# A two-stage attention and expert kernel: new order of loads and first chain, and batches with a Newton reciprocal and ScalarE's work in another order

## Chip, cores and metric

One Trainium2 chip, one of its cores. The metric is the device time of one execution in microseconds (us), the median of several runs. The engines are TensorE (PE), VectorE (DVE), ScalarE (ACT), GpSimd (POOL) and SyncE (SP), which only starts transfers here.

## The reference

Sixteen sequences of 512 tokens, 128 channels, all fp32. The first half is linear attention with random features, the second a feed-forward layer that sends each token to one of eight experts. Both are gated by rows made from a 16 x 128 condition.

```python
mod = silu(c) @ wmod                       # 6 rows per sequence: sa, ca, ga, sb, cb, gb
h = layernorm(x) * (1 + ca) + sa
q, k = feature(h @ Wq.T + bq), feature(h @ Wk.T + bk)   # exp(proj - norm) + 1e-6, 32 per head, 16 heads
kv, ksum = k.T @ v, sum(k)                 # per head
x = x + ga * ((q @ kv) / (q @ ksum) @ Wo.T + bo)
h = layernorm(x) * (1 + cb) + sb
e = argmax(h @ gate_W + gate_b)            # one expert of 8 per token
x = x + gb * (gelu(h @ W1[e] + b1[e]) @ W2[e] + b2[e])
```

The division by `q @ ksum` is the part of the arithmetic that the change writes in another way.

## The kernel before

Each engine has its own instruction list, written out by hand in program order, and waits on semaphores. There is no scheduler: an engine does its list in order, and whatever stands behind a waiting instruction waits too.

**Head.** SP starts the first loads (L324 to L332). ACT and DVE make silu of the condition (L494, L669 to L673), PE multiplies it with `wmod` (L973 to L976), DVE turns the products into columns `sa`, `ca1` (L685, L686) and rows `modrow` (L687 to L704), which go through DRAM and come back copied to all partitions as `modb` (L340, L335).

**Sixteen batches**, one for each sequence (`over_batches`, L89). In batch b:

- ACT (L546 to L572): four exponentials of the k features (`kf`, L531), with the copy of h2 of batch b-2 (`h2T`, L540), the copy of v (L527) and the copy of the gate logits (`lgT`, L544) among them; four exponentials of the q features (`qf`, L536), with the modulated input `hT` of batch b+1 (L509) after the second; k and its squares for batch b+1 (L516, L517), the copy `kvm` (L565), q and its squares (L522, L523), the denominator `den` (L570), and last the normalised input `xn1` of batch b+2 (four instructions, L503). In the profile `kvals`, `ksqs`, `hT`, v and `xn1` are all parts of one tile, `shared`.
- PE (L1125 to L1152): k features (L1016, L1019), transposes of h2 (L1084), v (L1000), gate (L1091), output projection of batch b-1 (L1076), q features (L1028, L1031), transposes of `xn1` of batch b+1 (L987), the key-value product (L1042, L1046), the k projection of b+1 (L995), ranks of b-2 (L1106 to L1109), two transposes (L1053), the q projection of b+1 (L995), and `attend` (L1060 denominator, L1064 numerator).
- DVE (L867 to L904): residual and statistics, expert choice and slots of b-2, scaling of h2 of b-1, and last `attention` (L718): a RECIPROCAL of `den` (L720), then `oT` = numerator times reciprocal (L723).
- POOL (L444 to L456): for even b the first layer norm's scale and shift of the pair b+2, b+3 (`rstd1_of`, L411 and L413), the second layer norm's scale of b-1 (`rstd2_of`, L419, which also waits for the gate rows of batch b-2), `gated` (L421: `wo`, `bog`, and the bias added to x, L427 to L434), which waits for `den` of batch b, and four indirect DMAs that scatter the rows of b-2 to lists of their experts in DRAM (L440).
- SP: gate rows of each batch copied into the payload tiles `pay` (`gate_rows`, L362, L366). They stand behind all loads of x, the late `modb` rows, `firsts`, `w2` and the padding (L343 to L352).

**Last batch.** PE first counts the tokens of the experts (`count`, L1117) and transposes a table of blocks (L1122) ahead of the q features; DVE makes that table (L868 to L872).

**Experts.** 71 blocks of 128 tokens: load, transpose (L1168), first product (L1175), gelu (L594), second product (L1188), bias, gate and residual on DVE (L921 to L926), and an indirect DMA out (L473). The last two batches' choice of experts runs among the first 32 blocks.

## Time and profile before

| what | value |
|---|---|
| median of 3 runs | 429.49 us (427.32 to 431.19) |
| the profiled execution's own time | 431.88 us |
| its span on the core | 430.0 us |
| busy share PE / DVE / ACT / POOL | 87% / 70% / 63% / 47% |
| granted clock of TensorE, mean | 0.97 |

The span is what the trace shows, from the first instruction to the last; 1.9 us of the execution's own time lie around it. The batches take roughly the stretch from 17 to 258 us, the experts the rest. Times in the views are microseconds from the start of the span unless marked ns. A busy PE is not PE at its peak, since matmuls are pipelined.

### The profile page before, as it was taken

Reading aid. Unit: us, or ns where it says so; the run is one execution under the profiler, and the core shown is the slowest. Engines: PE = TensorE matmul, PEld = TensorE weight load, DVE = VectorE, ACT = ScalarE, POOL = GpSimd, SP = SyncE. Lnnn points to the kernel's source line nnn. Section 1 sums busy time; section 2 is a strip of 40 time slices with the busy share of each in tenths; the row PEclk is TensorE's granted clock in tenths of the full one; section 3 lists DMA queues with packets and bytes.
Section 4 is the critical chain, followed back from the end, with each engine's and each line's share of the span. In section 5 each row is a group of like instructions: output and inputs, shape, how many; then the busy total and the mean of one; then the engine's idle time right before and its main releaser. Section 6 shows DMA issues by size and latency. Waiting matters only on the chain.

```text
span 430.0 us, 12990 instructions
## 1 busy us (share of the span) xinstructions
PE 373.3 (87%) x4487; PEld 284.5 (66%) x4487; DVE 300.8 (70%) x1106; ACT 272.9 (63%) x710; POOL 201.6 (47%) x226
## 2 busy tenths in 40 slices
PE   3598959999999999999999977998787899999990
PEld 1354636565655565565556537987787799999990
DVE  3536858987988898879867878777365566665651
ACT  2676754787687669667776726654554376657660
POOL 1210334553843664565546425455546354554452
PEclk9999998999999999999999989999898899999996
DMA  6458962112211221221122147344434455554410
GB/s 199 158 188 320 374 187 101 58 45 101 79 63 64 96 81 40 88 99 57 49 101 76 57 134 224 96 108 141 149 113 146 140 187 182 147 147 121 123 32 2
DMA packets 30782, 52.38 MB, mean 122 GB/s; under 512 B 4194, under 2 KB 22758, under 8 KB 30336
## 3 DMA queue, kind: packets, MB, share of 16 engines
q1 hardware_dynamic: 24352, 34.50, 26.5%
q0 software_dynamic: 6368, 17.05, 10.9%
q8 instruction: 38, 0.62, 0.6%
q14 instruction: 24, 0.20, 0.1%
HBM read 28.46 MB, written 19.34 MB: 111 GB/s over the span
## 4 chain that ended last, share of the span: by engine, by line
PE 55%; ACT 17%; DVE 13%; issue 7%; another core or an unknown queue 3%; DVEq 2%; DMA 1%; POOL 1%; POOLq 0%; SPq 0%; ACTq 0%
PE ps_proj L1188 10%; PE ps_feat L1175 6%; PE ps_proj L1028 4%; PE ps_proj L995 4%; DVE rden L720 4%; PE ps_out L1076 3%; PE ps_den L1060 3%; PE ps_proj L1031 3%; ACT kf L531 3%; PE ps_kv L1175 3%; PE ps_feat L1016 3%; PE ps_den L1175 3%; ACT qf L536 3%; ACT shared L516 2%
## 5 line engine op out<-in xcount | busy, mean ns | idle before, releaser
L473 POOL DMA_INDIRECT out<-kf,modb x71 | 70.6, 995 | 75.2 <-DVE kf L926 67.3
L1188 PE MATMUL ps_proj<-w2sb,qf 128*128 x568 | 77.1, 281 | 0.0
L440 POOL DMA_INDIRECT experts_lists<-pay,slot x64 | 63.5, 992 | 17.6 <-issue 17.6
L1188 PEld LDWEIGHTS ps_proj<-w2sb,qf 128*128 128x128 f32 x568 | 71.3, 197 | 0.0
L586 ACT ACTIVATE xT<-ps_out 128x128 f32<-128x128 f32 x71 | 19.7, 278 | 62.5 <-PE ps_out L1168 45.0
L720 DVE RECIPROCAL rden<-den 128x512 f32<-128x512 f32 x16 | 53.6, 3351 | 5.6 <-ACT den L570 5.3
L921 DVE TENSOR_TENSOR kf<-ps_proj,firsts_sb 128x128 f32<-128x128 f32 x71 | 20.7, 291 | 51.0 <-PE ps_proj L1188 22.9
L536 ACT ACTIVATE qf<-ps_proj 128x512 f32<-128x512 f32 x32 | 17.4, 595 | 45.8 <-PE ps_feat L1031 45.8
L427 POOL TENSOR_TENSOR wo<-wsb,modb 128x128 f32<-128x128 f32 x16 | 7.5, 469 | 82.3 <-ACT den L570 82.3
L1175 PE MATMUL ps_feat<-xT,shared 128*128 128x128 f32 x288 | 39.6, 281 | 5.4 <-ACT xT L586 3.6
L594 ACT ACTIVATE qf<-ps_feat,shared 128x128 f32<-128x128 f32 x144 | 41.0, 376 | 0.0
L1175 PEld LDWEIGHTS ps_feat<-xT,shared 128*128 128x128 f32 x288 | 35.9, 196 | 6.8 <-issue 6.2
L995 PE MATMUL ps_proj<-shared,wsb 128*128 128x512 f32 x64 | 34.2, 619 | 2.2 <-ACT shared L509 1.4
L861 DVE COPY shared<-firsts_sb 128x516 f32 x71 | 31.8, 448 | 2.5 <-issue 2.3
L1016 PEld LDWEIGHTS ps_feat<-feat_w,shared 32*128 32x128 f32 x256 | 19.7, 186 | 14.3 <-issue 14.2
L503 ACT ACTIVATE shared<-xall,shift,rstd 128x128 f32<-128x128 f32 x64 | 26.2, 481 | 4.0 <-POOL shift L413 4.0
L419 POOL TENSOR_TENSOR rstd<-ve,mhalf 128x4 f32<-128x4 f32 x16 | 16.6, 1036 | 25.1 <-DVE ve L621 11.9
L1016 PE MATMUL ps_feat<-feat_w,shared 32*128 32x128 f32 x256 | 26.7, 283 | 1.7 <-ACT qsqs L523 1.7
L1016 PE MATMUL ps_proj<-feat_w,shared 32*128 32x128 f32 x256 | 26.5, 283 | 0.0
L1175 PE MATMUL ps_den<-xT,shared 128*128 128x128 f32 x144 | 19.8, 282 | 6.4 <-ACT xT L586 3.5
L1019 PE MATMUL ps_feat<-csb,shared 32*128 32x128 f32 x256 | 25.1, 270 | 0.0
L1019 PE MATMUL ps_proj<-csb,shared 32*128 32x128 f32 x256 | 24.9, 270 | 0.0
(177 smaller groups left out, 965.1 us busy)
## 6 DMA issues: line engine op xcount, KB each, us to landing
modb<-experts_lists SPq DMA_DIRECT2D x71, 196.0 KB
xall<-in_x SPq DMA_DIRECT2D x16, 256.0 KB, 2.9
pay<-modb SPq DMA_DIRECT2D x16, 256.0 KB, 2.6
modb<-modulation_rows SPq DMA_DIRECT2D x1, 3072.0 KB, 11.0
firsts_sb<-in_firsts SPq DMA_DIRECT2D x1, 2576.0 KB, 16.9
experts_lists<-padding SPq DMA_DIRECT2D x9, 196.0 KB
out<-kf,modb POOLq DMA_INDIRECT x71
modb<-modulation_rows SPq DMA_DIRECT2D x1, 1024.0 KB, 5.1
```

The lines of the kernel that those rows point to most:

```text
L440: g_.indirect_dma_start(out=lists, in_=pay[b.home][:, t, :], in_offset=None, out_offset=bass.IndirectOffsetOnAxis(ap=slot[b.home][:, t:t + ...
L473: g_.indirect_dma_start(out=rows_out, in_=yb[u], in_offset=None, out_offset=bass.IndirectOffsetOnAxis(ap=token, axis=0), bounds_check=last ...
L503: ins = a.activation(xn1[:, t, :], xall[:, b.v * LT + t, :], ACT.Identity, bias=shift1[:, at:at + 1], scale=rstd1[:, at:at + 1])
L536: a.activation(qf[:, Q_ORDER[n], :], QB[Q_ORDER[n]][:, :], ACT.Exp).then_inc(s_exp, 1)
L594: ins = a.activation(g[k % R4][:, c * P:(c + 1) * P], HID[k % R4][:, c * P:(c + 1) * P], ACT.Gelu, bias=firsts_c[k % R4][:, WB1 + c:WB1 + ...
L720: v.reciprocal(rden[:], den[:]).then_inc(s_rden, 1)
L861: v.tensor_copy(firsts_c[k % R4], firsts_sb[:, bass.ds(expert[k] * WB, WB2)]).then_inc(s_fc, 1)
L995: mm(PJ[i][:, :], wsb[:, i * P:(i + 1) * P], hT[:], start=True, stop=True).then_inc(s_proj, 1)
L1016: mm(QB[c][:, tokens], kvals[at, tokens], feat_w[at, :], start=True, stop=False)
L1019: ins = mm(QB[c][:, tokens], ksqs[at, tokens], norm_w[at, :], start=False, stop=True)
L1175: ins = mm(HID[u % R4][:, c * P:(c + 1) * P], firsts_c[u % R4][:, c * P:(c + 1) * P], xT[u % 2][:], start=True, stop=True)
L1188: ins = mm(Y[u % 2][:, 0:D], g[u % R4][:, c * P:(c + 1) * P], w2sb[:, bass.ds(e * DFF + c * D, D)], start=(c == 0), stop=(c == FC - 1))
```

## The change

It has two halves. In the head: x of the first batch is loaded before the weights; PE runs 48 idle matmuls ahead of the condition's products and 12 more before the first projection; the column products come first and have a semaphore of their own; the first `xn1` is made half by ACT and half by DVE, the second by DVE alone; the first q projection goes into another bank, so that the first k features need no q; gate rows of batches 0 to 2 are copied before most loads of x, and `w2` is loaded last, behind the gate rows of batch 3.

In the batches: `den` becomes a logarithm, an exponential of its negative gives a first value of the reciprocal, and DVE makes one Newton step of it in two instructions (with the sign turned, so the residual subtracts). ACT makes `xn1` of batch b+1 after the four k exponentials of batch b, no longer that of b+2 at the end; `h2T` is copied one exponential earlier, `kvm` ahead of the squares of k. POOL's `rstd1_of` goes from the front of an even batch to its end. In the last batch count and table transpose go later on PE.

```diff
@@ sync @@
+            load_x(0, 0)
             sp.dma_start(wsb[:], weights).then_inc(s_w, 16)
-            load_x(0, 0)
...
-            with sp.Fori(EARLY_ROWS // 2, B // 2) as i:
-                for parity in range(2):
-                    sp.wait_ge(s_x[parity], 16 * i)
-                    load_x(2 * i + parity, parity)
+            load_x_behind(EARLY_ROWS)
+            load_x_behind(EARLY_ROWS + 1)
+            sp.wait_ge(s_mb, 16)
+            sp.wait_ge(s_pset, 2 + HOMES)
+            for v in range(HOMES):
+                gate_rows(v)
+            load_x_behind(EARLY_ROWS + 2)
+            load_x_behind(EARLY_ROWS + 3)
             load_rows(EARLY_ROWS, B, s_mbl)
+            for b in range(EARLY_ROWS + 4, B):
+                load_x_behind(b)
             sp.dma_start(firsts_sb[:], firsts).then_inc(s_w1, 16)
+            sp.wait_ge(s_pset, 3 + HOMES)
+            sp.dma_start(lists[PADROW:PADROW + P, :], padding[:]).then_inc(s_pad, 16)
+            sp.wait_ge(s_mbl, 16)
+            gate_rows(HOMES)
             sp.dma_start(w2sb[:, :].rearrange("p (e c d) -> p e c d", e=E, c=FC),
                          w2.rearrange("e (c p) d -> p e c d", p=P)).then_inc(s_w2, 16)
@@ gpsimd @@
-                if ahead and b.par == 0:
-                    rstd1_of(b.half + 3, b=b + 2)
                 if not first:
                     rstd2_of(b + -1, rows_of=None if second else b + -2)
                 gated(b, first)
                 if not first and not second:
                     scatter(b + -2)
+                if ahead and b.par == 0:
+                    rstd1_of(b.half + 3, b=b + 2)
@@ scalar @@
+            a.preload_act_table_set("natural_log_exp_and_others")
...
                 k_feature(b, 0)
-                k_feature(b, 1)
                 if not first and not second:
                     h2T_copy(b + -2)
+                k_feature(b, 1)
...
                 k_feature(b, 3)
+                if not first and not last:
+                    normalise1(b + 1)
                 q_feature(b, 0)
...
                 if not last:
-                    k_parts(b + 1)
-                act.wait_ge(s_kvt, b.v + 1)
-                a.activation(kvm[:], G[:, 0:2 * P], ACT.Copy).then_inc(s_kvm, 1)
+                    k_values(b + 1)
+                kvm_copy(b)
                 if not last:
+                    k_squares(b + 1)
                     q_parts(b + 1)
                 act.wait_ge(s_den, b.v + 1)
                 act.wait_ge(s_eps, b.v + 1)
-                a.activation(den[:], G[:], ACT.Identity, bias=kveps[:, 1:2]).then_inc(s_denp, 1)
-                if b.v + 2 < B:
-                    normalise1(b + 2)
+                a.activation(den[:], G[:], ACT.Ln, bias=kveps[:, 1:2]).then_inc(s_denp, 1)
+                act.wait_ge(s_denp, b.v + 1)
+                a.activation(rden[:], den[:], ACT.Exp, scale=-1.0).then_inc(s_rden, 1)
@@ vector @@
-                dve.wait_ge(s_denp, b.v + 1)
-                v.reciprocal(rden[:], den[:]).then_inc(s_rden, 1)
                 dve.wait_ge(s_rden, b.v + 1)
+                v.scalar_tensor_tensor(out=G[:], in0=G[:], scalar=kveps[:, 1:2], in1=rden[:],
+                                       op0=ALU.add, op1=ALU.mult).then_inc(s_rdst, 1)
+                dve.wait_ge(s_rdst, 2 * b.v + 1)
+                v.scalar_tensor_tensor(out=rden[:], in0=G[:], scalar=2.0, in1=rden[:],
+                                       op0=ALU.subtract, op1=ALU.mult).then_inc(s_rdst, 1)
@@ tensor @@
+            pe.wait_ge(s_set, 3)
+            keep_busy(48)
             pe.wait_ge(s_silu, 1)
...
-                if last:
-                    count(0)
                 k_features(b, first)
...
                 v_project(b)
+                if last:
+                    count(0)
...
-                if last:
-                    table_transpose(0)
...
                 if not last:
                     transpose_xn(b + 1, first)
+                else:
+                    table_transpose(0)
```

`load_x_behind(b)` waits until x of batch b-2 has landed and then loads x of b. `keep_busy(n)` issues n matmuls of 128 x 128 bf16 ones into an unused bank. `normalise1(b)` on ACT waits for `shift1_ready`, which POOL's `rstd1_of` raises.

On POOL, after the `den` of batch 2 (lines L427 and L440 are `gated` and the scatter, L411 and L413 `rstd1_of`, L419 `rstd2_of`), the list before reads:

```order
L427 TENSOR_TENSOR wo<-wsb,modb 128x128
L430 TENSOR_TENSOR bog<-rsb,modb 128x128
L434 TENSOR_TENSOR xall<-xall,bog 128x512
L440 DMA experts_lists<-pay,slot 66688x392 x4
L419 TENSOR_TENSOR rstd<-ve,mhalf 128x4
L427 TENSOR_TENSOR wo<-wsb,modb 128x128
L430 TENSOR_TENSOR bog<-rsb,modb 128x128
L434 TENSOR_TENSOR xall<-xall,bog 128x512
L440 DMA experts_lists<-pay,slot 66688x392 x4
L411 TENSOR_TENSOR rstd<-ve,mhalf 128x8
L413 TENSOR_TENSOR shift<-mv,rstd 128x8
```

and the list now, from the same place (L438 and L451 are `gated` and the scatter, L422 and L424 `rstd1_of`, L430 `rstd2_of`):

```order
L438 TENSOR_TENSOR wo<-wsb,modb 128x128
L441 TENSOR_TENSOR bog<-rsb,modb 128x128
L445 TENSOR_TENSOR xall<-xall,bog 128x512
L451 DMA experts_lists<-pay,slot 66688x392 x4
L422 TENSOR_TENSOR rstd<-ve,mhalf 128x8
L424 TENSOR_TENSOR shift<-mv,rstd 128x8
L430 TENSOR_TENSOR rstd<-ve,mhalf 128x4
L438 TENSOR_TENSOR wo<-wsb,modb 128x128
```

The pair of instructions of `rstd1_of` that stands behind the first scatter here makes scale and shift of batches 4 and 5. In the list before, that pair for batches 4 and 5 stands ahead of the first row shown, with one `rstd2_of` between them; the pair at the end of the first piece makes those of batches 6 and 7.

On ACT, from the two k exponentials out of `ps_proj` (the third and fourth) of a batch to the front of the next, before:

```order
L531 ACTIVATE kf<-ps_proj 128x4x128 x2
L536 ACTIVATE qf<-ps_proj 128x512 x2
L509 ACTIVATE shared<-ps_out,sa,ca 128x512
L536 ACTIVATE qf<-ps_feat 128x512 x2
L516 ACTIVATE shared<-ps_proj,wsb 128x512
L517 ACTIVATE shared<-ps_proj,wsb 128x512
L565 ACTIVATE kvm<-ps_den 128x256
L522 ACTIVATE qvals<-ps_proj,wsb 128x512
L523 ACTIVATE qsqs<-ps_proj,wsb 128x512
L570 ACTIVATE den<-ps_den,kveps 128x512
L503 ACTIVATE shared<-xall,shift,rstd 128x128 x4
```

and now:

```order
L550 ACTIVATE kf<-ps_proj 128x4x128 x2
L515 ACTIVATE shared<-xall,shift,rstd 128x128 x4
L555 ACTIVATE qf<-ps_proj 128x512 x2
L521 ACTIVATE shared<-ps_out,sa,ca 128x512
L555 ACTIVATE qf<-ps_feat 128x512 x2
L528 ACTIVATE shared<-ps_proj,wsb 128x512
L536 ACTIVATE kvm<-ps_den 128x256
L532 ACTIVATE shared<-ps_proj,wsb 128x512
L541 ACTIVATE qvals<-ps_proj,wsb 128x512
L542 ACTIVATE qsqs<-ps_proj,wsb 128x512
L591 ACTIVATE den<-ps_den,kveps 128x512
L593 ACTIVATE rden<-den 128x512
```

The four instructions that write `xn1` (`shared<-xall,shift,rstd`) went from behind `den` to the place between the k and the q exponentials, and are those of the next batch, no longer of the one after it; `kvm` changed places with the squares of k; `rden` is new.

## Rows read from the trace of the kernel before

**Rows 1.** ACT's timeline, first k exponential of batches 3, 4, 15: start, duration, instruction [idle before].

```profile
60.47 1.09 ACT L531 ACTIVATE kf<-ps_feat 128x512 f32<-128x512 f32 x2 [0.59 <-PE ps_proj L1019]
...
80.72 1.09 ACT L531 ACTIVATE kf<-ps_feat 128x512 f32<-128x512 f32 x2 [0.59 <-PE ps_proj L1019]
...
243.85 1.09 ACT L531 ACTIVATE kf<-ps_feat 128x512 f32<-128x512 f32 x2 [2.32 <-PE ps_proj L1019]
```

**Rows 2.** ACT's timeline inside batch 8.

```profile
142.27 1.08 ACT L531 ACTIVATE kf<-ps_proj 128x512 f32<-128x512 f32 x2
146.19 1.08 ACT L536 ACTIVATE qf<-ps_proj 128x512 f32<-128x512 f32 x2 [2.84 <-PE ps_feat L1031]
...
150.32 0.38 ACT L565 ACTIVATE kvm<-ps_den 128x256 f32<-128x256 f32 x1
...
151.15 0.71 ACT L523 ACTIVATE qsqs<-ps_proj,wsb 128x512 f32<-128x512 f32 x1
151.97 0.69 ACT L570 ACTIVATE den<-ps_den,kveps 128x512 f32<-128x512 f32 x1
152.56 1.64 ACT L503 ACTIVATE shared<-xall,shift,rstd 128x128 f32<-128x128 f32 x4
```

**Rows 3.** PE's timeline inside batch 8.

```profile
145.34 0.66 PE L987 MATMUL ps_out<-csb,shared 128*128 128x128 f32 x4
...
148.00 1.12 PE L995 MATMUL ps_proj<-shared,wsb 128*128 128x512 f32 x2
...
149.34 1.02 PE L995 MATMUL ps_proj<-shared,wsb 128*128 128x512 f32 x2
150.85 1.07 PE L1060 MATMUL ps_den<-qf,kvm 128*32 128x512 f32 x8 [0.48 <-ACT kvm L565]
```

**Rows 4.** DVE's timeline, `attention` of batch 7.

```profile
137.88 3.35 DVE L720 RECIPROCAL rden<-den 128x512 f32<-128x512 f32 x1
...
141.27 0.75 DVE L723 SCALAR_TENSOR_TENSOR oT<-ps_kv,kveps,rden 128x512 f32<-128x512 f32 x1
```

**Rows 5.** POOL's timeline, behind `den` of batch 7.

```profile
137.99 0.46 POOL L427 TENSOR_TENSOR wo<-wsb,modb 128x128 f32<-128x128 f32 x1 [5.81 <-ACT den L570]
...
140.38 1.06 POOL L440 DMA_INDIRECT experts_lists<-pay,slot  x1 [0.17 <-issue]
...
145.26 1.67 POOL L411 TENSOR_TENSOR rstd<-ve,mhalf 128x8 f32<-128x8 f32 x1
147.01 0.21 POOL L413 TENSOR_TENSOR shift<-mv,rstd 128x8 f32<-128x8 f32 x1
```

**Rows 6.** SP's, POOL's and PE's timelines at the long wait of batches 2 and 3.

```profile
36.92 18.66 SPq L352 DMA_DIRECT2D experts_lists<-padding  x1
...
60.58 1.01 POOL L419 TENSOR_TENSOR rstd<-ve,mhalf 128x4 f32<-128x4 f32 x1 [8.99 <-DMA pay<-modb]
...
64.28 1.05 PE L1084 MATMUL ps_gate<-csb,pay 128*128 128x128 f32 x4 [3.82 <-DVE pay L659]
```

**Rows 7.** Busy time by stretch there: length, PE, PEld, DVE, ACT, POOL, granted clock, DMA.

```profile
64.00:66.00 2.00, 1.72 (x9) 1.73 (x10) 2.00 (x2) 0.60 (x1) 1.69 (x2) 0.60 0.10 38
66.00:68.00 2.00, 1.62 (x13) 0.94 (x12) 1.97 (x2) 0.91 (x3) 1.49 (x2) 0.55 0.43 163
```

**Rows 8.** PE's timeline of the head.

```profile
6.54 1.44 PE L973 MATMUL ps_kv<-qf,silu 128*16 128x384 f32 x2 [6.54 <-DMA qf<-in_wmod]
...
9.19 0.61 PE L975 MATMUL ps_feat<-silu,qf 128*128 128x16 f32 x2
...
11.77 1.98 PE L995 MATMUL ps_proj<-shared,wsb 128*128 128x512 f32 x4 [0.93 <-ACT shared L509]
15.45 0.38 PE L1016 MATMUL ps_feat<-feat_w,shared 32*128 32x128 f32 x2 [1.70 <-ACT qsqs L523]
```

**Rows 9.** PE's timeline of the last batch, table transpose and q features.

```profile
248.66 0.56 PE L1122 MATMUL ps_den<-csb,tab 128*1 128x128 f32 x2 [1.40 <-DVE tab L833]
...
252.64 1.09 PE L1042 MATMUL ps_kv<-kf,shared 128*32 128x129 f32 x32
```

More of the change, by code:

```diff
@@ L569, in batch @@
                 act.wait_ge(s_eps, b.v + 1)
-                a.activation(den[:], G[:], ACT.Identity, bias=kveps[:, 1:2]).then_inc(s_denp, 1)
-                if b.v + 2 < B:
-                    normalise1(b + 2)
+                a.activation(den[:], G[:], ACT.Ln, bias=kveps[:, 1:2]).then_inc(s_denp, 1)
+                act.wait_ge(s_denp, b.v + 1)
+                a.activation(rden[:], den[:], ACT.Exp, scale=-1.0).then_inc(s_rden, 1)
             start, end = Batch(0), Batch(B)
-            normalise1(start)
+            act.wait_ge(s_shift1, 1)
+            for t in range(LT // 2):
+                ins = a.activation(xn1[:, t, :], xall[:, t, :], ACT.Identity,
+                                   bias=shift1[:, t:t + 1], scale=rstd1[:, t:t + 1])
+            ins.then_inc(s_xns, 1)
             act.wait_ge(s_cols, 1)
             modulate(start)
-            k_parts(start)
-            q_parts(start)
-            normalise1(start + 1)
+            k_values(start)
+            k_squares(start)
+            q_parts(start, bank=I)
             over_batches(batch)
@@ L886, in batch @@
                     table_rows(0)
-                if not first and not second:
+                    kv_values(b)
                     experts(b + -2)
-                kv_values(b, first)
-                if not first and not second:
-                    slots(b + -2)
+                elif not first and not second:
+                    experts(b + -2)
+                if not last:
+                    kv_values(b, first)
+                    if not first and not second:
+                        slots(b + -2)
                 if second:
@@ L967, in _, with keep_busy @@
             mm, tr = nc.tensor.matmul, nc.tensor.transpose
+            def keep_busy(n):
+                for _ in range(n):
+                    mm(PJ[1][:, 0:P], ones_bf[:], ones_bf[:], start=True, stop=True)
+            pe.wait_ge(s_set, 3)
+            keep_busy(48)
             pe.wait_ge(s_silu, 1)
@@ L1006, in k_features @@
                 pe.wait_ge(s_kst, 2 * (b.v + 1))
-                pe.wait_ge(s_qst, 2 * (b.v + 1))
-                if first:
-                    pe.wait_ge(s_bo, 1)
-                else:
+                if not first:
+                    pe.wait_ge(s_qst, 2 * (b.v + 1))
                     pe.wait_ge(s_exp, 2 * NC * b.v)
@@ L1146, in batch @@
                     project(b + 1, 0)
-                if not first and not second:
+                if not first and not second and not last:
                     rank(b + -2, first=third)
@@ L1156, in _ @@
             start, end = Batch(0), Batch(B)
+            pe.wait_ge(s_xns, 1)
             transpose_xn(start, first=True)
-            for i in range(2):
-                project(start, i, first=True)
+            keep_busy(12)
+            project(start, 0, first=True)
+            project(start, 1, first=True, bank=I)
             over_batches(batch)
```

95 lines of the change are left out of this document (60 added, 35 removed).

## The prediction

> **What bounds the kernel now.** I read the page first: PE is the busiest engine, but busy shares say little here, so I took ACT's timeline next and read off the start of the first k exponential of each batch. From batch 4 to batch 15 it moves by (243.85 - 80.72) / 11 = 14.83 us, as steady as a clock; the one step that is different is that from batch 3 to 4, 80.72 - 60.47 = 20.25 us [rows 1]. So the batches are one loop with a fixed period, and the question is which ring of waits closes it. The chain of waits, followed through one batch, runs k features (PE), kf, h2T and v (ACT), output projection and q features (PE), two q exponentials and `hT` (ACT), k projection (PE), k values, squares and `kvm` (ACT), `attend` (PE), and k features again. The reader should see three places in it.
>
> First, `attend` starts 0.15 us after `kvm` ends (150.32 + 0.38), though the q projection ahead of it on PE ended at 149.34 + 1.02 = 150.36 [rows 2, 3]: PE idles 0.48 us for `kvm`. Second, ACT has nothing to do for 2.84 us between the k and the q exponentials, because it waits for PE [rows 2]. Third, the RECIPROCAL (3.35 us) is the largest DVE instruction, but `oT` is out at 141.27 + 0.75 = 142.02 [rows 4], just when the copy of v, which the output projection also waits for, ends (the third k exponential starts at 142.27 with only the small `lgT` between [rows 2]). Two paths tie there, so a shorter reciprocal alone gives nothing.
>
> POOL looks idle enough (47%). What matters is when its work lies: it waits for `den` at the end of a batch, and only then come `wo`, the bias, four scatters and, in every second batch, `rstd1_of` [rows 5].
>
> **The change, part by part.**
>
> *Head.* The column products stood behind the two wide ones and began at 9.19; now they are first, when `wmod` has landed (6.54). The wide products follow with the clock already raised by the idle matmuls, the transposes start at an estimated 8.5 and the projections near 9.95 instead of 11.77. The k features began at 15.45, behind all four parts of k and q [rows 8]; without the two q parts (some 1.15 us) they begin near 12.5. Gain 2.95 us; 1.1 if only the q parts count, 3.5 at best.
>
> *Gate rows.* In batch 3 PE idled 3.82 us for h2 because POOL waited 8.99 us for gate rows, which stood behind the SP row of 18.66 us [rows 6]. Now these rows are copied early. The whole excess of that step goes: 20.25 - 14.83 = 5.42 us, with bounds of 3.82 and 5.42. SP is moved past a new wait: the gate rows of batch 3 wait for the scatter of batch 0, and `w2` with its long issue stands between them and those of batch 4. POOL needs the latter two to three batches later; 18.66 us fits into that, so I take nothing.
>
> *`kvm` ahead of the squares.* `attend` moves from 150.85 to about 150.40: 0.45 us a batch, 15 times, 6.75. Behind it, the q squares still end at 151.86 [rows 2], before `attend` does, so nothing new is late. *`h2T` one place earlier* meets transposes that have only just been issued; I take 0.12 us lost a batch, 14 times, 1.7, between 0 and 0.2 each.
>
> *Reciprocal.* ACT: `den` as logarithm, like the 0.69 now, and an exponential of one half of 1.09; DVE: two instructions like the one of 0.75 [rows 1, 2, 4]. From `den`'s start to `oT` that is 0.7 + 0.6 + 3 x 0.75 = 3.6 us instead of 4.8. `oT` is then 1.2 us ahead of v, off the chain, worth nothing directly. Each DVE instruction could take 1.2 / 3 = 0.4 us more before it cost anything. The added 0.6 us on ACT goes where `xn1` (1.64) was, and is hidden by PE's k features. If it were on the chain it would cost 15 x 0.6 = 9 us; bounds 0 and 9, and I take 0, since ACT had even with `xn1` 0.59 us to spare [rows 1].
>
> *Last batch.* PE waited 1.40 us for the table, and with a fallen clock the key-value product came at 252.64 [rows 9], 8.79 after the batch's first exponential; in batch 8, whose first exponential lies at 80.72 + 4 x 14.83 = 140.04, the product follows the transposes at 145.34 + 0.66 = 146.0, 5.96 after [rows 1, 3]. Both moves take that away, 2.8 us. The copies of the first expert weights and `oT` move with it. Bounds 1.4 and 3.
>
> Together without what follows: 2.95 + 5.42 + 6.75 - 1.7 + 2.8 = 16.2 us gained.
>
> ***The move of `rstd1_of` against that of `xn1`.*** `xn1` of batch b+1 goes into the idle 2.84 us, and there it fits (1.64). But it needs `shift1`, and for an even b+1 that is now made by POOL at the end of batch b's list, behind `gated` and four scatters. The pieces of the order above show exactly the run of instructions which batch 8 has in the trace: `wo` at 137.99, scatters from 140.38, `rstd1_of` at 145.26, shift done at 147.01 + 0.21 = 147.22 [rows 5]. This counts from the `den` of the batch before and will count the same. ACT wants it when the k exponentials are over, 142.27 + 1.08 = 143.35 [rows 2]. So ACT waits 3.9 us in front of `xn1`, with all q exponentials behind it in its list. `xn1` ends near 148.9, and PE, which has done its q features, transposes then instead of at 145.34 [rows 3]: 3.6 us, and 3.7 with the small shifts (`den` gains less than `attend` does). The key-value product and the k projection stand behind the transposes, so the whole ring is 3.7 us late. Before, the same shift had until 152.56, 5.3 us of slack.
>
> It happens for `xn1` of batches 4, 6, 8, 10, 12 and 14, six times; for batch 2 there is no scatter ahead of it, and the shift is just in time.
>
> PE idles through each of these waits. The trace has one idle like it: 3.82 us, and that step was 5.42 us longer, 1.6 more than the idle; the granted clock then was 0.60 and 0.55 for 4 us, near the 1.2 GHz level instead of 2.4 [rows 1, 6, 7]. I take 1.5 per wait, between 0 and 1.9. A wait costs 3.7 + 1.5 = 5.2 us, six of them 31.2.
>
> The Trainium skill says the same of the clock from the other side (TensorE: Matmul & The Clock Gate, Terms): the penalty is the time spent throttled times the share of pulses withheld. For the two stretches of rows 7 that would be 2 x 0.40 + 2 x 0.45 = 1.7 us, and the six waits 32.4 instead of 31.2. By that page's advice not to leave TensorE idle between bursts this change works against itself, since it warms the engine once in the head and cools it six times.
>
> Sum: -16.2 + 31.2 = +15.0 us. Against the profiled execution's own 431.9 that is 446.9; it was 2.4 above the median of the runs, and against 429.49 the sum gives 444.5, which I forecast.
>
> **The rivals.**
>
> *A. The waits come, the clock stays up.* Six times 3.7 is 22.2, less 16.2: +6, 435.5. For it: one idle of this length is little evidence for six. Against: the one idle of this length in the trace did lower it, and even the 1.40 us one was followed by slow ones: table transposes and q features took 252.64 - 248.66 = 4.0 us, and the q features take 145.34 - 143.35 = 2.0 in batch 8 [rows 2, 3, 9].
>
> *B. POOL keeps up, and it is faster.* If the shift is there before the k exponentials end, nothing is lost, and it is 429.49 - 16.2 = 413.3. The place is POOL's stretch from `wo` to shift, 9.2 us; the point from which it decides is a loss of 16.2 / 6 = 2.7 us a wait, so that stretch would have to shrink by more than 1 us where the clock stays up, and by 2.5 with the clock's part. For it: `rstd1_of` alone is 1.67 and may be shorter beside a less busy DVE. Against: each scatter occupies POOL for 0.96 and 0.30 of issue, with nothing in the change to shorten it.
>
> *C. Half and half.* The gains are larger than I sum (the ring of the batches gives 1 us each once `oT` is early) and the waits as in A: 425 to 433, no difference to be told.
>
> *D. More is late.* SP's new order holds gate rows of batch 4 behind `w2` (18.66 us of issue), or the exponential is not covered: 5 to 9 us more, 450 to 454.
>
> **How the numbers follow.** Forecast 0.56, A 0.16, B 0.12, C 0.09, D 0.07. The forecast's own range is 438 to 450. I let B fall out of the range mostly and take in A and part of C and D: 427 to 451. A measurement of this kernel can tell about 1% from no change, 425.2 to 433.8. Slower by more: the forecast, D and most of A, 0.76. Within: C's larger part and a little of A, 0.10. Faster: B and the rest, 0.14.
>
> **What would show it.** In the profile after, ACT should wait for POOL's shift some 3.9 us ahead of the first of four `xn1` in batches 3, 5, 7, 9, 11 and 13, at the top of the list of waits; the periods should alternate, some 14.5 and 19.7; the granted clock should fall below 1 six times, right after those waits. The first k features should start near 12.5, and the step from batch 3 to 4 should be like the other odd ones. The forecast is wrong if the periods are even, if the shift is ready by the end of the k exponentials, or if the first features come no earlier than 15.45.

## The result, and the profile after

The changed kernel takes 448.12 us (median of 4 runs, 446.41 to 451.01), the kernel before 430.34 beside it: ratio 1.043, 95% interval 1.035 to 1.051. It is slower by 4.3%. The profiled execution took 447.48 us, its span is 445.7 with a mean granted clock of 0.959; before, 431.88, 430.0 and 0.972. Executions fall into a faster and a slower state, and all ratios are taken from the runs in the faster one, so a median of all runs can lie above what its ratio says.

ACT's timeline of the changed kernel (start, duration, instruction, idle time before it), the first k exponential of batches 0, 3, 4, 5, 9, 10 and 15:

```profile
15.14 0.60 ACT L550 ACTIVATE kf<-ps_feat 128x512 f32<-128x512 f32 x1 [0.98 <-PE ps_proj L1073]
56.25 0.60 ACT L550 ACTIVATE kf<-ps_feat 128x512 f32<-128x512 f32 x1 [1.14 <-PE ps_proj L1073]
76.88 0.60 ACT L550 ACTIVATE kf<-ps_feat 128x512 f32<-128x512 f32 x1 [1.14 <-PE ps_proj L1073]
91.47 0.60 ACT L550 ACTIVATE kf<-ps_feat 128x512 f32<-128x512 f32 x1 [1.14 <-PE ps_proj L1073]
...
160.01 0.60 ACT L550 ACTIVATE kf<-ps_feat 128x512 f32<-128x512 f32 x1 [1.14 <-PE ps_proj L1073]
179.70 0.60 ACT L550 ACTIVATE kf<-ps_feat 128x512 f32<-128x512 f32 x1 [1.14 <-PE ps_proj L1073]
...
262.26 0.60 ACT L550 ACTIVATE kf<-ps_feat 128x512 f32<-128x512 f32 x1 [1.14 <-PE ps_proj L1073]
```

The steady step of 14.83 us [rows 1] is gone. From an odd batch to an even one the step is now 19.7 (179.70 - 160.01), 20.6 from batch 3 to 4, from an even to an odd one 14.6 (91.47 - 76.88). What follows is one of the long steps. First the list of waits (us in total, times, longest), then POOL's, ACT's and PE's timelines in batch 9:

```profile
ACT shared L515 <- POOL shift L424: 25.8, 6, 4.4
```

```profile
158.35 0.46 POOL L438 TENSOR_TENSOR wo<-wsb,modb 128x128 f32<-128x128 f32 x1 [5.72 <-ACT den L591]
...
165.63 1.67 POOL L422 TENSOR_TENSOR rstd<-ve,mhalf 128x8 f32<-128x8 f32 x1
167.38 0.21 POOL L424 TENSOR_TENSOR shift<-mv,rstd 128x8 f32<-128x8 f32 x1
```

```profile
162.22 1.12 ACT L550 ACTIVATE kf<-ps_proj 128x512 f32<-128x512 f32 x2
167.62 1.65 ACT L515 ACTIVATE shared<-xall,shift,rstd 128x128 f32<-128x128 f32 x4 [4.27 <-POOL shift L424]
169.17 1.05 ACT L555 ACTIVATE qf<-ps_proj 128x512 f32<-128x512 f32 x2
```

```profile
164.91 0.59 PE L1087 MATMUL ps_feat<-qsqs,csb 32*128 32x512 f32 x2
169.32 0.66 PE L1043 MATMUL ps_out<-csb,shared 128*128 128x128 f32 x4 [3.81 <-ACT shared L515]
169.91 1.92 PE L1099 MATMUL ps_kv<-kf,shared 128*32 128x129 f32 x32
171.59 1.94 PE L1103 MATMUL ps_kv<-kf,ones 128*32 128x128 f32 x32
...
174.81 1.02 PE L1051 MATMUL ps_proj<-shared,wsb 128*128 128x512 f32 x2
175.76 1.06 PE L1117 MATMUL ps_den<-qf,kvm 128*32 128x512 f32 x8
```

Read them from the top. POOL goes through the same nine microseconds as before (158.35 to 167.59, compare [rows 5]); ACT has finished its k exponentials and stands 4.27 us for the shift; PE has finished its q features and stands 3.81 us for ACT. The reader should then look at the durations: the two halves of the key-value product take 1.92 and 1.94, where the first half took 1.09 in the last batch before [rows 9]. That is the clock, as the stretches show (length, PE, PEld, DVE, ACT, POOL, granted clock, DMA):

```profile
168.00:170.00 2.00, 0.68 (x8) 0.52 (x12) 0.00 (x0) 2.00 (x6) 0.55 (x1) 1.00 0.44 131
170.00:172.00 2.00, 2.00 (x40) 1.96 (x44) 0.00 (x0) 1.86 (x4) 0.00 (x0) 0.50 0.04 8
172.00:174.00 2.00, 2.00 (x34) 1.34 (x25) 0.41 (x3) 0.00 (x0) 0.00 (x0) 0.65 0.00 0
```

From 174 on it is 1.00 again. Behind the first wait, in batch 3, it stays down twice as long: 0.54, 0.50, 0.50 and 0.75 in the four stretches from 64 to 72 us.

The last two rows of PE's piece show that `attend` follows the q projection without a gap (174.81 + 1.02 to 175.76): the 0.48 us for `kvm` [rows 3] are gone.

The spans differ by 15.7 us, and the first k exponentials split that up. Until batch 0: 17.50 to 15.14, 2.4 gained. Batches 0 to 3: 42.97 to 41.11, 1.9 gained. From 3 to 4: 20.25 to 20.63, so one wait went and another took its place, 0.4 lost. From 4 to 15: 163.13 to 185.38, 22.25 lost. Behind that 186.15 to 183.44, 2.7 gained.

The head, PE's timeline:

```profile
1.13 5.22 PE L1022 MATMUL ps_proj<-ones_bf 128*128 128x128 bf16 x48 [1.13 <-DVE seen L692]
6.76 0.37 PE L1029 MATMUL ps_feat<-silu,qf 128*128 128x16 f32 x2 [0.40 <-DMA qf<-in_wmod]
...
7.59 0.82 PE L1033 MATMUL ps_kv<-qf,silu 128*16 128x384 f32 x2
...
10.58 1.12 PE L1051 MATMUL ps_proj<-shared,wsb 128*128 128x512 f32 x2 [0.27 <-ACT shared L521]
```

A pair of wide products takes 0.82 us, where it took 1.44 [rows 8]. That the clock is the reason is read off these durations alone: the profile prints a granted clock of 1.00 for the whole head of both kernels. The first projection starts at 10.58, 1.2 us earlier than before.

### The profile page after: what moved, and what is told of

Same layout as the page of the kernel before. It is cut to its first block, busy times and chain, and to the rows that moved or that the text cites. A ratio compares the mean times of both kernels' runs of the same rounds, so it can differ in the third digit from the quotient of the medians.

```text
span 445.7 us, 13088 instructions
## 1 busy us (share of the span) xinstructions
PE 381.2 (86%) x4547; PEld 294.2 (66%) x4547; DVE 270.5 (61%) x1128; ACT 277.8 (62%) x720; POOL 201.6 (45%) x226
## 4 chain that ended last, share of the span: by engine, by line
PE 57%; ACT 16%; POOL 12%; issue 6%; another core or an unknown queue 4%; DMA 3%; DVE 1%; SPq 1%; POOLq 0%; DVEq 0%; ACTq 0%
PE ps_proj L1249 11%; PE ps_feat L1236 7%; POOL experts_lists L451 6%; PE ps_proj L1051 6%; PE ps_den L1236 3%; PE ps_kv L1099 3%; PE ps_kv L1236 3%; PE ps_kv L1103 3%; ACT kf L550 2%; POOL rstd L422 2%; ACT shared L515 2%; PE ps_proj L1084 2%; PE ps_feat L1070 2%; PE ps_out L1133 2%
## 5 line engine op out<-in xcount | busy, mean ns | idle before, releaser
L451 POOL DMA_INDIRECT experts_lists<-pay,slot x64 | 63.8, 997 | 19.1 <-issue 17.4
L438 POOL TENSOR_TENSOR wo<-wsb,modb 128x128 f32<-128x128 f32 x16 | 7.3, 457 | 117.5 <-ACT den L591 117.5
L611 ACT ACTIVATE xT<-ps_out 128x128 f32<-128x128 f32 x71 | 19.7, 278 | 63.1 <-PE ps_out L1229 37.2
L515 ACT ACTIVATE shared<-xall,shift,rstd 128x128 f32<-128x128 f32 x56 | 23.2, 504 | 25.8 <-POOL shift L424 25.8
L750 DVE SCALAR_TENSOR_TENSOR kvT<-ps_kv,csb 128x128 f32<-128x128 f32 x16 | 5.7, 356 | 51.9 <-PE ps_kv L1103 51.0
L1043 PE MATMUL ps_out<-csb,shared 128*128 128x128 f32 x64 | 11.0, 297 | 23.0 <-ACT shared L515 23.0
L1043 PEld LDWEIGHTS ps_out<-csb,shared 128*128 128x128 f32 x64 | 7.0, 145 | 35.4 <-ACT shared L515 29.5
L550 ACT ACTIVATE kf<-ps_feat 128x512 f32<-128x512 f32 x32 | 18.9, 596 | 18.0 <-PE ps_proj L1073 18.0
```

The lines of the kernel that those rows point to most:

```text
L451: g_.indirect_dma_start(out=lists, in_=pay[b.home][:, t, :], in_offset=None, out_offset=bass.IndirectOffsetOnAxis(ap=slot[b.home][:, t:t + ...
L515: ins = a.activation(xn1[:, t, :], xall[:, b.v * LT + t, :], ACT.Identity, bias=shift1[:, at:at + 1], scale=rstd1[:, at:at + 1])
L550: a.activation(kf[:, :, c, 0:P], QB[c][:, :].rearrange("p (t m) -> p t m", t=LT), ACT.Exp)\
L611: a.activation(xT[u % 2][:], XT[:, 0:P], ACT.Copy).then_inc(s_bT, 1)
```

## The experiments

The runs fell on chips of two kinds. On two of them the kernel before takes 429 to 430 us, on one 412. So a run is compared by its ratio to the kernel before, measured beside it on the same chip, and between chips only by steps (the time from one first k exponential to that of the next batch).

### Is it the place of `rstd1_of`?

`e_front` puts the call back to the front of POOL's even batch; all else stays as changed. `e_ahead` puts it between `gated` and the scatters, `e_two` between the second and the third scatter.

```diff
 e_front
+                if ahead and b.par == 0:
+                    rstd1_of(b.half + 3, b=b + 2)
                 if not first:
                     rstd2_of(b + -1, rows_of=None if second else b + -2)
                 gated(b, first)
                 if not first and not second:
                     scatter(b + -2)
-                if ahead and b.par == 0:
-                    rstd1_of(b.half + 3, b=b + 2)
 e_two
                 if not first and not second:
-                    scatter(b + -2)
+                    scatter(b + -2, [0, 1])
                 if ahead and b.par == 0:
                     rstd1_of(b.half + 3, b=b + 2)
+                if not first and not second:
+                    scatter(b + -2, [2, 3])
```

> The changed kernel with one thing undone: rstd1_of stands at the front of an even batch on POOL again. Theory (six waits of ACT for POOL's shift, 5.05 us each with the fallen clock): the waits are gone, every period from batch 4 on is 14.1 to 14.6, and the time is 448.1 - 30 = 418 us (415 to 421), well below before. Rival 1 (the place of xn1 or the added exponential slows the ring by itself, and the waits only show it): 430 or more. Rival 2 (POOL's second scale is late instead, as it now stands behind rstd1_of): waits of DVE for rstd2, periods above 15, 422 to 430.

Measured: 415.71 us, ratio 0.967 (0.963 to 0.972), span 415.4. The six waits are out of the list of waits and the long steps with them:

```profile
129.09 0.60 ACT L550 ACTIVATE kf<-ps_feat 128x512 f32<-128x512 f32 x1 [1.13 <-PE ps_proj L1073]
...
143.71 0.60 ACT L550 ACTIVATE kf<-ps_feat 128x512 f32<-128x512 f32 x1 [1.13 <-PE ps_proj L1073]
...
157.90 0.60 ACT L550 ACTIVATE kf<-ps_feat 128x512 f32<-128x512 f32 x1 [1.14 <-PE ps_proj L1073]
```

Steps of 14.62 and 14.19 in turn. The place of `rstd1_of` is worth 1.043 - 0.967 = 0.076 of the time, some 32 us, and without its move the change is a gain of 3.3%.

> The changed kernel with rstd1_of between gated and the four scatters of the same batch. Theory (the scatters' 5 us are what makes the shift late): it is ready some 4.2 us after wo begins, 1 us before ACT asks, no wait, and 418 us as with e_front; the scatters lie 2 us later in every second batch and nobody waits for them. Rival (it is too late already because it stands behind den of the batch before): waits of 1 to 2 us stay in odd batches, 425 to 432. Rival (late scatters delay the payload's reuse or the gate rows): waits of DVE or SP for scatters, 422 or more.

Measured: 423.52 us, ratio 0.987 (0.982 to 0.991). ACT no longer waits for the shift, and yet it is 2% slower than `e_front`: a miss, taken up below.

> The changed kernel with two of the four scatters behind rstd1_of, so that two stay ahead of it: half the dose. The shift comes 2 x 1.27 = 2.5 us earlier; ACT should wait 4.27 - 2.53 = 1.7 us and PE idle 3.81 - 2.53 = 1.3 us, six times. Theory with the clock falling only after the long idle: 6 x 1.3 = 8 above e_front, 426 us. If TensorE's clock falls after the short idle as well: 6 x 2.7 = 16 above it, 434 us. Rival (cost not proportional to the wait): as e_front or as the changed kernel.

Measured: 421.47 us, ratio 0.980 (0.976 to 0.985). That is 5.8 us above `e_front`, where 8 had been expected. The list of waits has the wait at less than half its length:

```profile
ACT shared L517 <- POOL shift L424: 10.5, 6, 1.9
```

The long steps are 15.48 us (the first 15.62), 1.29 above the 14.19 of `e_front`, though ACT waits 1.9 at most. So a wait of that length costs less than itself: what counts is how long PE stands, 1.28 us in batch 9. The granted clock is 1.00 in all stretches from 20 to 236 us, so it does not fall here: a single idle of 1.40 us in the kernel before was followed by slow products [rows 9], the six here of 1.27 to 1.41 were not.

### Is a part of it the clock?

`e_warm` keeps all six waits, and fills PE's idle time in them with 64 matmuls of ones, whose output the transposes overwrite.

```diff
             def transpose_xn(b, first=False):
+                if not first and b.v in (4, 6, 8, 10, 12, 14):
+                    pe.wait_ge(s_x2, b.v - 1)
+                    for _ in range(64):
+                        mm(H[:, 0:P], ones_bf[:], ones_bf[:], start=True, stop=True)
                 pe.wait_ge(s_xn1, b.v + 1)
```

> The changed kernel with 64 idle matmuls (128 x 128, bf16, into the free bank of the transposes) on PE in each of the six waits, ahead of the wait for xn1; they take about 3.6 us at the full clock and end before xn1 does. The waits of ACT stay as they are. Theory (1.3 of the 5.05 us of a wait is the lowered clock): granted clock 1.00 behind the waits, key-value product 2.0 us instead of 3.5, 448.1 - 6 x 1.4 = 440 us (438 to 442). Rival (the clock has no share, the loss is all waiting): 448.

Measured: 437.74 us, ratio 1.019 (1.014 to 1.023). ACT's six waits are there in full (25.9 us), but PE's timeline in batch 9 and the stretch at the key-value product read:

```profile
159.52 3.75 PE L1040 MATMUL ps_out<-ones_bf 128*128 128x128 bf16 x64
...
164.00 1.09 PE L1103 MATMUL ps_kv<-kf,shared 128*32 128x129 f32 x32
```

```profile
164.00:166.00 2.00, 2.00 (x66) 1.80 (x66) 0.00 (x0) 1.96 (x4) 0.00 (x0) 1.00 0.00 0
```

The long steps are 18.04 us instead of 19.65, and the first of them 18.18 instead of 20.63. That splits a wait: 18.04 - 14.19 = 3.9 us are the wait, 19.65 - 18.04 = 1.6 us the clock; in the first one, where the clock stayed down twice as long, it is 20.63 - 18.18 = 2.45. In ratios the clock is 1.043 - 1.019 = 0.025, 10.6 us, 1.8 a wait. The time PE stands can be filled with work that computes nothing, and a third of the loss comes back (0.025 of 0.076).

### What are the parts of the batch half worth?

Each of these four takes `e_front` and undoes one more edit. They ran on the 412 us chip.

```diff
 e_recip  (ScalarE and VectorE as before, RECIPROCAL on DVE)
-                a.activation(den[:], G[:], ACT.Ln, bias=kveps[:, 1:2]).then_inc(s_denp, 1)
-                act.wait_ge(s_denp, b.v + 1)
-                a.activation(rden[:], den[:], ACT.Exp, scale=-1.0).then_inc(s_rden, 1)
+                a.activation(den[:], G[:], ACT.Identity, bias=kveps[:, 1:2]).then_inc(s_denp, 1)
...
+                v.reciprocal(rden[:], den[:]).then_inc(s_rden, 1)
...
 e_kvm
-                kvm_copy(b)
                 if not last:
                     k_squares(b + 1)
+                kvm_copy(b)
 e_h2T
-                if not first and not second:
-                    h2T_copy(b + -2)
                 k_feature(b, 1)
+                if not first and not second:
+                    h2T_copy(b + -2)
 e_xnlast
-                if not first and not last:
-                    normalise1(b + 1)
                 q_feature(b, 0)
...
                 a.activation(rden[:], den[:], ACT.Exp, scale=-1.0).then_inc(s_rden, 1)
+                if b.v + 2 < B:
+                    normalise1(b + 2)
```

> e_front (the changed kernel with rstd1_of at the front again) with the division as before: den by Identity, RECIPROCAL on DVE, no exponential. Theory of the prediction (in the kernel before, oT and the copy of v tie, and the Newton step takes oT off the chain without gain): with kvm earlier the den-to-oT path is 0.2 to 0.4 us longer than the path by v, so 15 x 0.3 = 4 to 5 us above e_front. Rival 1 (worth nothing): within 1 us of e_front. Rival 2 (DVE's reciprocal bounded the ring): 15 x 1.2 = 18 us above e_front.

> e_front with kvm copied behind the squares of k again. Theory: attend starts 0.45 us later in each batch, 15 times, 6.75 us above e_front. Rival (the ring moves on to the q squares or the copy of v, so kvm's place gives nothing): within 1 us.

> e_front with the copy of h2T behind the second k exponential again. Theory of the prediction (0.12 us lost per batch to transposes only just issued): 1.7 us below e_front. Rival (in the changed kernel's trace the way from the first k exponential to the q features is 3.49 us against 3.43 before, 0.06): 0.9 us below, too little to tell. Rival (a gain): above e_front.

> e_front with xn1 made two batches ahead at the end of ACT's batch again, behind den and the exponential. Theory: xn1 (1.64) behind the exponential (0.63) ends about 0.5 us after the k features, so each batch from 1 to 13 is 0.3 to 0.5 us longer: 4 to 6 us above e_front; the move of xn1 paid for the exponential. Rival (there is room for both): within 1 us of e_front.

Measured: `e_recip` ratio 0.973 (0.969 to 0.977), `e_kvm` 0.981 (0.977 to 0.985), `e_h2T` 0.966 (0.962 to 0.970), `e_xnlast` 0.964 (0.960 to 0.967). `e_front` did not run on that chip, but its undisturbed step, which it has on its own (from batch 2 to 3, 13 to 14 and 14 to 15), is 14.14 us. The steps, each the same from batch 4 to 14 within 0.02: `e_kvm` 14.69, `e_recip` 14.38, `e_xnlast` 14.29, `e_h2T` 14.08, and 14.62 with the batches wholly as before (`e_head` and `e_gates`, below). First k exponentials of batches 8 and 9 in `e_kvm`, then in `e_h2T`:

```profile
130.37 0.60 ACT L550 ACTIVATE kf<-ps_feat 128x512 f32<-128x512 f32 x1 [1.46 <-PE ps_proj L1074]
...
145.05 0.60 ACT L550 ACTIVATE kf<-ps_feat 128x512 f32<-128x512 f32 x1 [1.47 <-PE ps_proj L1074]
```

```profile
126.18 0.60 ACT L550 ACTIVATE kf<-ps_feat 128x512 f32<-128x512 f32 x1 [1.13 <-PE ps_proj L1073]
...
140.25 0.60 ACT L550 ACTIVATE kf<-ps_feat 128x512 f32<-128x512 f32 x1 [1.13 <-PE ps_proj L1073]
```

So `kvm` ahead of the squares is worth 0.55 us a batch; the earlier `h2T` loses 0.06; the Newton step is worth 0.24, as PE's timeline of `e_recip` shows, where the output projection waits 0.72 us for `oT`, and for v 0.51 in `e_front`:

```profile
146.34 1.16 PE L1127 MATMUL ps_out<-wo,oT 128*128 128x128 f32 x8 [0.72 <-DVE oT L760]
```

The expectation for `e_xnlast`, 4 to 6 us above `e_front`, failed. The move of `xn1` gains 0.15 us a batch in the step, and in the total nothing (0.964 is the best ratio of all runs, though `e_h2T` reaches to 0.962). The clock blurs these totals: the mean granted clock of the six executions is 0.988 to 0.994 in `e_xnlast` and 0.981 to 0.986 in `e_h2T`, where it is 0.57 from 240 to 248 us, behind the batches. Singly undone, the edits sum to 0.55 - 0.06 + 0.24 + 0.15 = 0.88 us, more than the 0.48 (14.62 - 14.14) that the batch gained in all, so these prices don't add. Probably one edit cannot deliver while another is missing; no run undoes two of them to show it.

Totals say less than steps here. What lies behind batch 15 is nearly the same work in all kernels, and took 185.8 us in `e_front` (415.4 - 229.6) and 180.7 in `e_ahead2` (420.0 - 239.3); on the other chip 166.2 in `e_xnlast` and 170.4 in `e_h2T`.

### The head half alone, and the gate rows alone

`e_head` has the changed head and the new order of loads, with everything in the batches as before. `e_gates` is the kernel before with one edit, the gate rows of batches 0 to 2 copied ahead of most loads of x (the loop of these loads is written out, its waits are the same).

```diff
 e_gates
+            sp.wait_ge(s_mb, 16)
+            sp.wait_ge(s_pset, 2 + HOMES)
+            for v in range(HOMES):
+                sp.dma_start(pay[v][:, :, GT:GT + D],
+                             modb[:, v:v + 1, GB, :].to_broadcast([P, LT, D])).then_inc(s_gb[v], 16)
-            with sp.Fori(EARLY_ROWS // 2, B // 2) as i:
-                for parity in range(2):
-                    sp.wait_ge(s_x[parity], 16 * i)
-                    load_x(2 * i + parity, parity)
+            for b in range(EARLY_ROWS, B):
+                sp.wait_ge(s_x[b % 2], 16 * (b // 2))
+                load_x(b, b % 2)
...
-            sp.wait_ge(s_mb, 16)
-            for v in range(HOMES):
-                gate_rows(v)
             sp.wait_ge(s_mbl, 16)
```

> The head's half alone: the changed kernel's loads, first chain and gate rows, with the batches, the reciprocal, POOL's order and the last batch as before. Theory: the head gives 2.4 us (first k exponential 15.14 instead of 17.50 in the changed kernel's trace), the gate rows 5.4 us (the step from batch 3 to 4), so 430.3 - 7.8 = 422.5 us. Rival (the gate rows' wait is replaced by another): the step stays above 17 and the time above 426.

> The kernel before with one edit: the gate rows of batches 0 to 2 are copied as soon as their modulation rows have landed, ahead of the other loads of x. Theory: the step from batch 3 to 4 falls from 20.25 to 14.8, and the time by 5.4 to 425 us. Rival (w2 or the late rows hold the next gate rows instead, or the loads of x come late): less than 3 us.

Measured: `e_head` 404.43 us, ratio 0.983 (0.978 to 0.987); `e_gates` 409.67, 0.990 (0.986 to 0.994). Both as expected. In `e_gates` the step from batch 3 to 4 is 14.62 like all others, so the whole excess went with the gate rows. The ratios give 4.3 us of 412 for the gate rows and 7.2 for the head with them.

The trace of `e_gates` shows something else that matters for the price of the head. Its head is that of the kernel before, and yet its first k exponential comes at 21.89 instead of 17.50. PE's transposes, from `before` and then from `e_gates`:

```profile
10.23 0.60 PE L987 MATMUL ps_out<-csb,shared 128*128 128x128 f32 x4
```

```profile
10.94 1.06 PE L988 MATMUL ps_out<-csb,shared 128*128 128x128 f32 x4
```

So the old head comes out 4.4 us apart in the two traces that have it, and the doubled durations point to the clock, though no printed clock shows it. All twelve traces with the changed head have the first k exponential at 14.1 to 15.6 us. One trace of the kernel before can't price what the idle matmuls are worth.

### Why is `e_ahead` slower than `e_front`?

In the trace of `e_ahead` the six long steps are 15.67 us. PE's and POOL's timelines in batch 9:

```profile
153.01 1.16 PE L1099 MATMUL ps_kv<-kf,shared 128*32 128x129 f32 x31
...
155.37 1.12 PE L1103 MATMUL ps_kv<-kf,ones 128*32 128x128 f32 x31 [1.08 <-issue]
```

```profile
153.56 0.97 POOL L451 DMA_INDIRECT experts_lists<-pay,slot  x1 [0.30 <-issue]
```

PE stands 1.08 us in the middle of a product, and the profile has nothing that it waits for ("issue"). So it does in the other odd batches from 5 to 13, and in batch 3 twice for less, 0.42 and 0.46. The stop ends 0.84 us after the end of POOL's fourth scatter (153.56 + 0.97). The kernel before has one in a place that I had passed over: ACT's q exponential starts at 146.19 after an idle of 2.84 us [rows 2]. POOL's fourth scatter there, and in batches 8 and 9 of `e_front`, stands like this (POOL and ACT of `before`, then of `e_front`):

```profile
144.28 0.96 POOL L440 DMA_INDIRECT experts_lists<-pay,slot  x1 [0.30 <-issue]
146.19 1.08 ACT L536 ACTIVATE qf<-ps_proj 128x512 f32<-128x512 f32 x2 [2.84 <-PE ps_feat L1031]
```

```profile
133.75 0.96 POOL L451 DMA_INDIRECT experts_lists<-pay,slot  x1 [0.30 <-issue]
...
135.66 1.08 ACT L555 ACTIVATE qf<-ps_proj 128x512 f32<-128x512 f32 x2 [1.73 <-PE ps_feat L1087]
...
148.36 0.96 POOL L451 DMA_INDIRECT experts_lists<-pay,slot  x1 [0.30 <-issue]
149.22 0.60 ACT L555 ACTIVATE qf<-ps_proj 128x512 f32<-128x512 f32 x1 [0.67 <-PE ps_feat L1087]
150.28 0.60 ACT L555 ACTIVATE qf<-ps_proj 128x512 f32<-128x512 f32 x1 [0.46 <-PE ps_feat L1087]
```

Each time an instruction starts 0.95 to 0.96 us after the fourth scatter's end: 146.19, 135.66, 150.28. In the odd batches of `e_front` the first q exponential starts 2.0 us after PE's q features and only the second is late; in its even ones the first starts 3.1 us after them, and in every batch of `before` 2.8. On the 412 us chip it is 2.0 in every batch, and no such stop is seen (`e_h2T`, batch 8: scatter to 131.78, exponential at 131.62).

The trace of `e_two` has a case against the fourth scatter as such. In its batch 9 that scatter ends as late as in `e_ahead`, 7.5 us behind the first k exponential, and 0.84 to 0.96 us after its end PE goes on without a stop, in the same product:

```profile
153.49 0.96 POOL L451 DMA_INDIRECT experts_lists<-pay,slot  x1 [0.30 <-issue]
```

```profile
155.19 1.06 PE L1105 MATMUL ps_kv<-kf,ones 128*32 128x128 f32 x32
```

The projection behind it starts at 156.18, as soon as the product is through. What differs is that `rstd1_of` stands between the second and the third scatter there. In the even batches of `e_two` the four scatters are in a row, and the q exponential is late again. So in these traces the stops go with four scatters in a row, and not with a late fourth one. The last two runs took `e_front` and `e_ahead` again, on one chip.

> The same kernel as the run e_front, again, beside the next one. In that run and in the kernel before ACT's first q exponential starts 2.0 us after PE's q features in some batches and 3.1 us after in others, and the late ones all start 0.95 us after the end of POOL's fourth scatter. The runs made on the other chip (kernel before 412 us) show 2.0 in every batch. Theory: something stops ACT and PE for about 1 us behind the fourth scatter on the first chip and not on the second. If this run falls on a chip of the second kind: every step from batch 3 on 14.1 us, none of 14.6, and 394 us where the kernel before has 412 (14.6 to 14.1 over twelve steps 5.8 us, gate rows and head 7.8, first steps and last batch 4): ratio 0.957. On a chip of the first kind: steps of 14.2 and 14.6 in turn and ratio 0.967, as before. It also gives the base that the four runs with one edit undone lacked on their chip.

> The same kernel as the run e_ahead, again. There it was 8 us above e_front, all of it in six steps of 15.67 us in place of 14.19, in each of which PE stood still for 1.08 us within the kv product, with nothing waited for, just behind POOL's fourth scatter. If that stop is the first chip's alone: on a chip of the second kind this kernel and e_front2 are within 1 us of each other and no step is above 14.2. If the order of POOL's work is the cause by itself (a later scatter or a later wo holds something): 6 to 8 us above e_front2 on any chip, with the six steps at 15.6.

Measured: `e_front2` 415.27 us, ratio 0.965 (0.961 to 0.969); `e_ahead2` 423.29, 0.984 (0.980 to 0.988). The chip was a third one, of the first kind (kernel before 429.2). The steps are 14.2 and 14.6 in `e_front2`, 15.6 to 15.7 and 14.6 in `e_ahead2`, PE's stop in its batch 9 is 1.12 us. So the difference is real, and it sits in the six long steps, with PE's stops at the same place on two chips. `rstd1_of` between `gated` and the scatters moves the fourth scatter from 5.6 us behind the first k exponential (149.32 - 143.71) to 7.5 (154.53 - 147.00), and there the stop hits PE's key-value product. At 5.6 it hits ACT's second q exponential, which had time: that step is 14.19 us, against 14.14 without a stop. The two did not run on a chip of the other kind, so whether they would be alike there is open, and so is what the stop is: the profile names no cause.

## Why the prediction was right

Predicted 444.5 us in a range of 427 to 451, measured 448.12. The base drifted by 0.85 of these 3.6 us; the forecast difference was +15.0, the measured one +15.7 by span and some 18 by the medians.

*The wait for the shift: right in its place, number and size.* Predicted 3.9 us of ACT ahead of `xn1` in six odd batches; the list of waits has 25.8 us, six times, 4.3 each. Predicted 3.7 for PE, 3.81 in its row. `e_front` shows that this wait is the cause: without it 1.043 becomes 0.967.

*The clock: right.* Predicted 1.5 us a wait out of one earlier idle; `e_warm` measures 1.6 by steps (2.45 in the first wait), 1.8 by ratios. Together 5.2 predicted and 5.5 measured (19.65 - 14.19), but 6.4 in the first (20.63 - 14.19): 33.7 in all instead of 31.2. Rival A (clock up, 435.5) is what `e_warm` made: 437.74. By the Trainium skill (TensorE: Matmul & The Clock Gate, Terms) the rows of batch 9 give 2 x 0.50 + 2 x 0.35 = 1.7 us, and the measured 1.6 agrees with that rule within 0.1. For batch 3 the rule gives 2 x (0.46 + 0.50 + 0.50 + 0.25) = 3.4 us, and the step lost 2.45 by the clock, so there the runs don't agree with it. PE was busy for only 0.31 us of the first of these four stretches, so little of the low clock there can have cost anything. It also means that the step from batch 3 to 4 is not like the other odd ones, as the prediction had it, but 1.0 us longer.

*The gains: 16.2 predicted, 14.5 measured*, by `e_front` and `e_front2` (1 - 0.966 of 430). Rival B named 413.3 for the kernel without the wait; `e_front` and `e_front2` took 415.71 and 415.27.

The spans of `before` and `e_front` say where the gain lies: 3.0 us until the first k exponential (17.50 - 14.49), 0.2 from batch 0 to 3 (42.97 - 42.79), 6.1 from 3 to 4 (20.25 - 14.19), 5.0 from 4 to 15 (163.13 - 158.11), 0.3 behind that (186.15 - 185.82). The batches' 5.0 meets the predicted 6.75 - 1.7 partly by luck: other parts than those two bring it about, as follows.

- Head 2.95: 2.4 in the trace after, 2.1 to 3.0 in its variants on chips of the same kind. The first k features started at 13.06 where I had 12.5, the first k exponential came at 15.14; the projections started at 10.58 where I had 9.95, since the wide products and `hT` between them were under-estimated.
- Gate rows 5.42: right, that step lost its whole excess in `e_gates` (14.62 like its neighbours; 4.3 us in the ratio, interval 2.7 to 6.0). In the changed kernel it can't be seen, because the new wait took the same step: 20.25 became 20.63; in `e_front` it is 14.19.
- `kvm` 0.45 a batch: 0.55. `h2T` 0.12 lost: 0.06.
- Reciprocal 0: 0.24 a batch gained, 3.4 us in all. The step that failed here is "two paths tie, so a shorter reciprocal alone gives nothing". In the kernel before they tied; with `kvm` earlier and the old reciprocal (`e_recip`), `oT` is the later of the two. A shorter reciprocal without the other edits was not run. ACT's exponential was hidden, as predicted.
- Last batch 2.8: from the first k exponential to the key-value product 268.00 - 262.26 = 5.74 us, before 8.79, so 3.05. In the totals little of it can be seen: behind the first k exponential of batch 15 the changed kernel is 2.7 us shorter than the kernel before and `e_front` 0.3.

PE's timeline there, to lay beside [rows 9]:

```profile
268.00 1.34 PE L1099 MATMUL ps_kv<-kf,shared 128*32 128x129 f32 x29
```

What I had wrong without harm: these per-batch terms were added as if each were free of the others. Singly undone they come to 0.88 us a batch, and together they gained 0.48 in an undisturbed step. My terms came to 0.45 - 0.12 = 0.33.

*D*, the queue of SP, didn't come. The prediction feared for it 18.66 us of issue of `w2`, but that row belongs to the padding [rows 6]; `w2` has a row of 0.89 us in the trace before and 0.79 now. The gate rows of batch 4 are issued 21 us after it starts, and the list of waits says what SP waits for there, the scatters (L350 are the gate rows):

```profile
SPq L350 <- DMA experts_lists<-pay,slot: 199.1, 12, 20.5
```

```profile
64.72 0.79 SPq L373 DMA_DIRECT2D w2sb<-in_w  x1
85.56 0.64 SPq L350 DMA_DIRECT2D pay<-modb  x1
```

No engine waits for these gate rows.

## What to carry to other kernels

When a consumer is moved to an earlier place in its engine's list, look up its producer's place in the other engine's list and count from the event which that list itself waits for: here POOL's 9.2 us from `den` to shift decided, and POOL's busy share of less than half said nothing. The price of such a wait on TensorE is the wait and the clock after it, here 3.9 + 1.6 us. And a change of two halves should be timed in halves: one function in the wrong place hid a gain of 3.3%; `e_front`, the changed kernel with that call back at the front, beats both kernels.

## What the runs showed that I had not expected

- On the chips where the kernel before takes 430 us, one engine stands for about 1.1 us and goes on 0.84 to 0.96 us after the end of the fourth indirect scatter, where the four stand in a row. On ACT it cost 0.4 to 0.5 us in each even batch (steps of 14.6 against 14.14 to 14.19), on PE 1.5. Behind the first three scatters of a batch nothing like it was found, nor behind the fourth where `rstd1_of` parts them two and two (`e_two`).
- Such stops are not bound to these scatters alone. In the expert stage each of the eight traces from chips of that kind has PE or ACT standing for 1.0 us or more with nothing waited for (2.05 and 4.70 in `before`, 2.55 and 3.93 in `e_front`). The six traces from the 412 us chip have none above 0.8 on PE or ACT behind the head. The cause stays open.
- Chips differ more in one stage than in others: the undisturbed step of the batches agrees between them, but what follows batch 15 takes 181 to 186 us on two and 166 to 170 on one. There `e_front` on the slower chip has PE busy for 14.03 of 20 us in one stretch; in `e_h2T` at about the same place it is 19.14. Part of that is the two stops just named (2.55 on PE, 3.93 on ACT), and the granted clock is 0.91 instead of 1.00:

```profile
284.00:304.00 20.00, 14.03 (x111) 13.82 (x112) 8.51 (x30) 9.10 (x36) 9.79 (x11) 0.91 0.41 125
```

```profile
280.00:300.00 20.00, 19.14 (x175) 18.88 (x174) 14.31 (x59) 12.74 (x50) 14.14 (x15) 1.00 0.62 178
```

- A wait of 1.9 us on ACT (`e_two`) cost 1.3 us and left the granted clock at 1.00; one of 4.3 us cost 5.5. Four microseconds of idle PE cost 1.6 us beyond themselves, and matmuls that compute nothing took that back.
- A warmed head is no guarantee. In `e_front`, `e_front2` and `e_ahead2` the step from batch 0 to 1 is 15.1 us instead of 13.4. PE is busy for 0.68 us between 16 and 18 us in `e_front`, and the granted clock is 0.88, 0.50 and 0.77 in the three stretches from 16 to 22. In the changed kernel PE is busy for 0.24 us there and the clock stays at 1.00, so the same idle does not lower it in every execution.
